# A transformer layer on one core: the start of the program is put in another order, and the first sequence's k leaves through ScalarE's queue

## Chip, cores and metric

The kernel runs on one core of one Trainium2 chip. The metric is the device time in microseconds of one execution; lower is better. A core has five engines that run side by side and meet only at semaphores: TensorE (PE; its weight loads are listed as PEld), VectorE (DVE), ScalarE (ACT), GpSimd (POOL) and SyncE (SP), which here only issues DMAs. Every engine executes its own instructions strictly in the order in which they are written, so a wait holds up all that stands behind it on that engine.

## What is computed

One adaLN transformer layer over x of shape (16, 512, 128), that is 16 sequences b of 512 tokens with 128 features. The reference, cut to what matters:

```python
mod = (silu(c) @ wmod).reshape(16, 6, 1, -1)          # sa, ca, ga, sb, cb, gb, one set per sequence
ga, gb = clamp_abs(ga, 0.25), clamp_abs(gb, 0.25)      # sign kept
h = layernorm(x) * (1 + ca) + sa
q, k, v = h @ wq.T + bq, h @ wk.T + bk, h @ wv.T + bv  # 16 heads of 8
scores = q k^T * 8**-0.5, only |i - j| <= 32
x = x + ga * (softmax(scores) @ v @ wo.T + bo)
h = layernorm(x) * (1 + cb) + sb
top 2 of 8 experts by softmax(h @ gate_w.T); experts and one shared: (silu(h s w1) * (h s w3)) @ w2
x = x + gb * (sum over the experts)
```

## The kernel before

**Stages.** The work goes sequence by sequence. Attention of sequence b runs beside the experts of sequence b-2. `fill()` holds by hand the order of all instructions of sequences 0 to 4 (with the experts of 0 to 2), `body(b, par)` is the repeated order for b = 5 to 11, `drain()` is the rest. Each engine has its own three lists, written out call by call, and nothing reorders them at run time.

**The prologue** stands ahead of `fill()`. SP issues eight loads of weights and of x (lines 282 to 288 and `load_x(0)` at 294), then the experts' weights w13 and w2 (lines 431, 432), then `load_x(1)`. The first seven share one semaphore `w_in`, and whoever needs one of them waits for all seven (112). From the condition `ct` ACT makes a tanh (line 1138), DVE makes silu from it (`cth` line 1671, `csl` line 1673), PE multiplies it with `wmod` (lines 2638 and 2641), DVE writes `mod` (lines 1680, 1681), PE multiplies that with the projection weights (line 2644), and DVE makes the biases `bqk` and `bvs` of all sequences (lines 1874 to 1876). DVE also forms the low parts `wql` of the split weights (lines 1675, 1676), and from lines 1878 to 1890 `mrow`, the rows of ga, gb and ga*bo, which go to DRAM (`put_rows`, lines 427, 428) and come back broadcast over the partitions as `brow`, `arow`, `grow` (lines 302, 310, 318).

**The first layernorm.** `statistics` (line 1691) and `moments` (line 1701) on DVE, `spread_var`, `inverse`, `shift`, `normal` on POOL (lines 665, 674, 680, 706), `flip` on PE (line 2659), `high_h1` on ACT (line 1160), `low_h1` on DVE (line 1707). Then PE projects q, k, v, each as three products of high and low parts (lines 2622 to 2624). ACT writes the high parts `qh`, `kh` (lines 1169, 1176), DVE the low parts `ql`, `kl` (lines 1717, 1725).

**Rearrangement of q and k through DRAM.** `put_q`, `put_ql`, `put_k`, `put_kl` (lines 327, 336, 345, 354) store them to `q_scr` and `k_scr`; `load_q` (line 364, four DMAs) and `load_k` (line 380, three DMAs) bring them back as `q4` and `k4`, for blocks 0 to 7 (h = 0) and 8 to 15 (h = 1) of the sequence apart. `load_q` waits until all three q stores have landed, `load_k` until all three k stores have, and the first ones also until the unused rows of `q4` are zero (`z_in`). Rows 96 to 127 of `q4` hold ones (`ones_q`, line 767, once for each h), and those of `k4` hold the window mask.

**Attention.** For each block n of 32 queries: `scores` on PE (line 2697), `maximum` on DVE (line 1738), `probabilities` on ACT (line 1184), `turn_p` on DVE (line 1755), `values` on PE (line 2720). Two score banks alternate. `add_bias` on POOL (line 696) needs `brow`. `warm(n)` on PE issues n matmuls whose result is not used (line 2629).

**Experts.** `scaled` (line 737) and `scaled_low` (line 743) on POOL, `scaled_high` (line 1206) on ACT, `expert` on PE, `half_silu` (line 1835) and `combine` (line 1844) on DVE, `down` on PE (line 2765). `expand_v` (line 715) on POOL spreads v.

## Time and profile before

| what | value |
|---|---|
| median of 3 runs | 700.81 us (695.68, 700.81, 701.35) |
| the profiled execution, its own time | 696.14 us |
| the profiled execution, its span | 694.1 us |
| PE busy | 653.3 us, 94% of the span |
| DVE, ACT, POOL busy | 599.7, 554.5, 566.2 us (86%, 80%, 82%) |
| DMA | 127.79 MB, mean 184 GB/s |

The time of an execution is its span and some 2 us around it (696.14 against 694.1). The span begins with the first instruction and ends with the last. The profile gives for every instruction its start and its duration; a bracket behind a row says how long the engine stood idle before it, and what ended that. Of a DMA the profile shows how long its issue took on the queue and, for some, how long it was from issue to landing. The granted clock of TensorE is 1.00 at 2.4 GHz and 0.50 at 1.2 GHz.

### The profile page before, as it was taken

The page shows a single profiled execution, that of the slowest core. Times are in us where ns is not written, and L with a number is a line of the kernel's source. Part 1 is how long each engine was busy: PE and PEld are TensorE (multiplying, and loading weights), DVE is VectorE, ACT ScalarE, POOL GpSimd, SP SyncE. Part 2 cuts the span into 40 slices and gives each one's busy share as a digit, 9 for nine tenths or more (in the row PEclk, how much of TensorE's full clock was granted, in tenths as well). Part 3 has the DMA queues.
Part 4 walks back from the last instruction along what each step waited for, and adds up shares of the span by engine and source line. Part 5 has one row for each costly group of instructions (what it writes and reads, how often), then busy time and mean ns, then how long its engine had stood idle before and what let it go on. Part 6 is the DMA issues. An engine that isn't in the chain of part 4 may idle for free. (4 is left out here: it accounts for less than half of the span.)

```text
span 694.1 us, 19396 instructions
## 1 busy us (share of the span) xinstructions
PE 653.3 (94%) x6075; PEld 560.8 (81%) x6075; DVE 599.7 (86%) x1568; ACT 554.5 (80%) x2458; POOL 566.2 (82%) x667
## 2 busy tenths in 40 slices
PE   6488889999999999999999999999999999999897
PEld 5277777888888888888888888888888888887685
DVE  6737778999898989999999999899989999897685
ACT  3258787989888888989898889899899898986352
POOL 6430619999988979899998989898999999898684
PEclk8669988999999999999999999999999999999999
DMA  5567788786787787786878777887868787633231
GB/s 175 157 143 192 164 211 219 197 232 165 178 241 196 202 219 190 189 231 159 224 205 227 190 201 205 228 201 191 201 190 210 207 209 221 157 101 99 77 129 31
DMA packets 193862, 127.79 MB, mean 184 GB/s; under 512 B 110640, under 2 KB 170720, under 8 KB 193632
## 3 DMA queue, kind: packets, MB, share of 16 engines
q1 hardware_dynamic: 193760, 126.56, 69.2%
q8 instruction: 48, 0.79, 0.5%
q14 instruction: 54, 0.44, 0.2%
HBM read 96.36 MB, written 30.17 MB: 182 GB/s over the span
## 5 line engine op out<-in xcount | busy, mean ns | idle before, releaser
L1184 ACT ACTIVATE p<-ps_s,nmx 128x96 f32<-128x96 f32 x1024 | 330.9, 344 | 34.9 <-DVE nmx L1738 33.0
L1184 ACT ACTIVATION_READ_ACCUMULATOR p<-ps_s,nmx 128x1 f32 x1024 | 216.2, 211 | 0.0
L737 POOL TENSOR_TENSOR xs<-h,sbc 128x512 f32<-128x512 f32 x128 | 165.5, 1300 | 18.9 <-DMA sbc<-s_scr 17.6
L1738 DVE TENSOR_REDUCE nmx<-ps_s 128x4 f32<-128x384 f32 x256 | 137.2, 548 | 37.0 <-PE ps_s L2697 36.8
L2697 PEld LDWEIGHTS ps_s<-k,q 128*128 128x128 f32 x1024 | 140.1, 197 | 34.1 <-DMA k<-k_scr 14.2
L743 POOL TENSOR_TENSOR xl<-xs,xh 128x512 fp32r<-128x512 f32 x120 | 153.4, 1283 | 17.2 <-ACT xh L1206 17.1
L2697 PE MATMUL ps_s<-k,q 128*128 128x96 f32 x1024 | 145.4, 277 | 18.7 <-DMA k<-k_scr 13.3
L2765 PE MATMUL ps_Y<-w2s,g 128*128 128x128 f32 x1152 | 153.5, 279 | 0.4 <-DVE g L1844 0.4
L2765 PEld LDWEIGHTS ps_Y<-w2s,g 128*128 128x128 f32 x1152 | 140.4, 192 | 5.6 <-DVE g L1844 0.8
L1755 DVE STREAM_TRANSPOSE pt<-p 128x384 f32<-128x384 f32 x256 | 133.5, 551 | 0.8 <-ACT p L1184 0.3
L1206 ACT ACTIVATE xh<-xs 128x512 fp32r<-128x512 f32 x128 | 79.9, 636 | 34.0 <-POOL xs L737 33.5
L1835 DVE SCALAR_TENSOR_TENSOR th<-th,ps_A 128x512 f32<-128x512 f32 x136 | 91.7, 674 | 15.1 <-ACT th L1227 13.9
L1227 ACT ACTIVATE th<-ps_A 128x512 f32<-128x512 f32 x136 | 82.5, 607 | 24.5 <-PE ps_A L2624 23.3
L1844 DVE TENSOR_TENSOR g<-th,ps_B 128x512 f32<-128x512 f32 x136 | 91.9, 676 | 1.7 <-PE ps_B L2624 0.3
L2622 PE MATMUL ps_A<-xh,w13h 128*128 128x512 f32 x136 | 63.3, 466 | 2.0 <-DVE th L1835 1.0
L2720 PE MATMUL ps_O<-pt,vd 128*32 128x96 f32 (+2 forms) x2304 | 64.4, 243 | 0.0
L715 POOL TENSOR_TENSOR vd<-vt,bmask 128x1024 f32<-128x1024 f32 x32 | 60.6, 1896 | 0.5 <-DVE vt L1733 0.5
L2622 PE MATMUL ps_B<-xh,w13h 128*128 128x512 f32 x136 | 55.3, 407 | 2.6 <-DVE g L1844 2.6
L2720 PEld LDWEIGHTS ps_O<-pt,vd 128*32 128x32 f32 x2304 | 44.2, 111 | 16.3 <-issue 6.0
L2624 PE MATMUL ps_B<-xl,w13h 128*128 128x512 f32 x136 | 53.7, 395 | 0.0
L2624 PE MATMUL ps_A<-xl,w13h 128*128 128x512 f32 x136 | 53.7, 395 | 0.0
L2623 PE MATMUL ps_A<-xh,w13l 128*128 128x512 f32 x136 | 53.6, 394 | 0.0
(138 smaller groups left out, 1010.8 us busy)
## 6 DMA issues: line engine op xcount, KB each, us to landing
sbc<-s_scr SPq DMA_DIRECT2D x64, 512.0 KB, 6.2
k<-k_scr SPq DMA_DIRECT2D x64, 384.0 KB
q<-q_scr SPq DMA_DIRECT2D x128, 96.0 KB
k<-k_scr SPq DMA_DIRECT2D x32, 336.0 KB
q_scr<-qh SPq DMA_DIRECT2D x32, 256.0 KB, 3.7
k_scr<-kh SPq DMA_DIRECT2D x32, 256.0 KB, 2.9
xr<-x SPq DMA_DIRECT2D x16, 256.0 KB, 3.1
q_scr<-ql SPq DMA_DIRECT2D x16, 256.0 KB, 3.7
```

What stands on the lines that cost most here:

```text
L737: nc.gpsimd.tensor_tensor(xs[:, n % 2], h2[:, par], sbc[:, n - 1], ALU.mult).then_inc(xs_d, 1)
L743: nc.gpsimd.tensor_tensor(xl[:, n % XRING], src, xh[:, n % XRING].bitcast(F32), ALU.subtract).then_inc(xl_d, 1)
L1184: last = nc.scalar.activation(p[:, n % PRING, gg, :], ps_s[:, n % 2, MK * gg:MK * gg + MK], ACT.Exp, bias=nmx[:, n, gg:gg + 1], accum_out= ...
L1738: nc.vector.tensor_reduce(nmx[:, n, :], ps_s[:, n % 2, 0:ACC].rearrange("p (g k) -> p g k", g=HG), AX.X, ALU.max, negate=True).then_inc(mx ...
L1755: nc.vector.transpose(pt[:, n % TRING].rearrange("p g r q -> p (g r q)"), p[:, n % PRING].rearrange("p g k -> p (g k)")).then_inc(tr_d, 1)
L1835: nc.vector.scalar_tensor_tensor(th[:, par], th[:, par], 1.0, banks(b, n)[0], ALU.add, ALU.mult).then_inc(v_d, 1)
L1844: nc.vector.tensor_tensor(g[:, par], th[:, par], banks(b, n)[1], ALU.mult).then_inc(g_d, 1)
L2622: mm(dst, wh, xh, start=True, stop=False)
L2624: return mm(dst, wh, xl, start=False, stop=True)
L2697: last = mm(ps_s[:, n % 2, MK * gg:MK * gg + MK], heads[:, h, gg, nl], k4[:, h, gg, :, MB * nl:MB * nl + MB], start=gg == 0, stop=gg == HG ...
L2720: last = mm(ps["O"][r, MB * n0:MB * n0 + MB * cnt], vd[:, kb, gg].rearrange("p j d -> p (j d)"), src, start=kb == 0 and run is runs[0], st ...
L2765: last = mm(ps["Y"][:, QB * a:QB * a + QB], g[:, par, QB * a:QB * a + QB], w2s[:, e, :], start=n == 0 and a == 0, stop=n == NX - 1, skip_g ...
```

## The change

Nothing is computed in another way. In the prologue SP loads `ct` first, then the first x, `wmod` and the projection weights, each with a semaphore of its own (`ct_in`, `x_in[0]`, `wm_in`, `wq_in`); the four small ones keep `w_in`, whose full count is 64 now. ACT makes the tanh and the high parts of the weights before the window mask, and `ones_q` is split: POOL writes it for h = 0 behind the first layernorm, ACT for h = 1 behind the k stores. DVE takes the statistics of the first x ahead of the condition, and makes the rows `mrow` (`make_rows`) after the first projections. The zeroing of `q4` is shared: DVE does half of h = 0, POOL the other half and all of h = 1. The memset of the middle of `k4` stands behind `low_h1(0)`. PE issues 8 matmuls on `ident` where it issued 14.

On SP `put_rows` moves from ahead of the first q store to behind the first loads of q4 and k4. `put_k(0, 0)` and `put_kl(0, 0)` leave SP; ACT issues the same three DMAs in their place (`send_k`, `send_kl`). For sequences 1 to 4 neighbours in the hand-written lists of all five engines trade places, and the `warm` calls of PE are set anew: 96 warm matmuls in `fill` where there were 107 (the first eight ahead of `project_v(0)` and those of the prologue stay). `body` and `drain` are unchanged.

The diff, cut to its core (the reordered neighbours of sequences 1 to 4 are left out but for a few):

```diff
...
-            sp.dma_start(wqf, wqkv).then_inc(w_in, 16)
-            sp.dma_start(ct[:], cT).then_inc(w_in, 16)
-            sp.dma_start(wm, wmod).then_inc(w_in, 16)
+            sp.dma_start(ct[:], cT).then_inc(ct_in, 16)
+            sp.dma_start(xr[:, 0], x[0:1].rearrange("o (a p) d -> p (o a) d", p=128)).then_inc(x_in[0], 16)
+            sp.dma_start(wm, wmod).then_inc(wm_in, 16)
+            sp.dma_start(wqf, wqkv).then_inc(wq_in, 16)
...
-                    sp.wait_ge(z_in[h], 1)
+                    sp.wait_ge(z_in[h], 2 - h)
...
-                    sp.wait_ge(z_in[0], 1)
+                    sp.wait_ge(z_in[0], 2)
...
-            load_x(0)
             sp.dma_start(w13f, w13).then_inc(e_in, 16)
             sp.dma_start(w2f, w2).then_inc(e_in, 16)
             load_x(1)

             def fill():

-                put_rows()
+                load_x(2)
                 put_q(0, 0)
                 put_ql(0, 0)
-                put_k(0, 0)
-                put_kl(0, 0)
                 load_q(0, 0, 0)
                 load_k(0, 0, 0)
+                put_rows()
                 load_bias(0)
                 load_ga(0)
                 load_q(0, 1, 0)
                 load_k(0, 1, 0)
-                load_gb(0)
-                load_bias(1)
-                load_x(2)
                 put_q(1, 1)
...
-            ones_q(0)
+            spread_var(0, l1, ln1)
+            inverse(0, l1, ln1)
+            shift(0, l1, ln1)
+            normal(0, l1, ln1)
+            pool.wait_ge(l1["xn"], NQB)
+            ones_q()
             const(nc.gpsimd.memset(bmask[:], 1.0))
             keep(bmask[:], [[-32, HJ]], 0, 1, val=0.0)
             keep(bmask[:], [[32, HJ]], 31, -1, val=0.0)
             const(nc.gpsimd.iota(iota8[:], [[1, NE]], base=0, channel_multiplier=0,
                                  allow_small_or_imprecise_dtypes=True))
-            ones_q(1)
-            spread_var(0, l1, ln1)
-            inverse(0, l1, ln1)
-            shift(0, l1, ln1)
-            normal(0, l1, ln1)
+            nc.gpsimd.memset(q4[0:KROWS, 0, 2:4].bitcast(F32), 0.0).then_inc(z_in[0], 1)
+
+            def clear_q():
+
+                nc.gpsimd.memset(q4[0:KROWS, 1].bitcast(F32), 0.0).then_inc(z_in[1], 1)

             def fill():

-                spread_var(1, l1, ln1)
                 expand_v(0, 0)
                 expand_v(0, 1)
+                clear_q()
+                spread_var(1, l1, ln1)
+                inverse(1, l1, ln1)
+                shift(1, l1, ln1)
                 add_bias(0)
-                inverse(1, l1, ln1)
+                normal(1, l1, ln1)
                 gate_wo(0)
...
+                scaled_low(0, 0, 0)
                 route_both(0)
                 route_weights(0)
-                scaled_low(0, 0, 0)
+                expand_v(2, 0)
...
+            act.wait_ge(ct_in, 16)
+            nc.scalar.activation(cth[:], ct[:], ACT.Tanh, scale=0.5).then_inc(s_th, 1)
+            act.wait_ge(wq_in, 16)
+            nc.scalar.activation(wqh[:, 0], wqf[:, 0], ACT.Copy, scale=SCALE)
+            nc.scalar.activation(wqh[:, 1:3], wqf[:, 1:3], ACT.Copy).then_inc(s_wh, 1)
...
+            def ones_q():
+
+                act.wait_ge(cst, IDENT)
+                nc.scalar.activation(q4[KROWS:128, 1].rearrange("p g n j q -> p (g n j) q"),
+                                     ident[KROWS:128, KROWS:128].unsqueeze(1).to_broadcast([MB, HG * HB * HJ, MB]),
+                                     ACT.Copy).then_inc(q_one[1], 1)
+
+            def send_k(b, par):
+
+                act.wait_ge(k_h, b + 1)
+                for role in (0, 1):
+                    nc.scalar.dma_start(k_scr[par, :, role].rearrange("j r s -> r j s"),
+                                        kh[:].bitcast(F32)).then_inc(k_scr_w, 16)
+
+            def send_kl(b, par):
+
+                act.wait_ge(k_l, b + 1)
+                nc.scalar.dma_start(k_scr[par, :, 2].rearrange("j r s -> r j s"), kl[:].bitcast(F32)).then_inc(k_scr_w, 16)
...
+                copy_w2()
+                send_k(0, 0)
+                send_kl(0, 0)
+                ones_q()
                 copy_w13()
-                copy_w2()
...
-            nc.vector.memset(q4[0:KROWS, 0].bitcast(F32), 0.0).then_inc(z_in[0], 1)
-            nc.vector.memset(k4[KROWS:128, :, :, 1].bitcast(F32), 0.0)
-            dve.wait_ge(s_th, 1)
-            nc.vector.scalar_tensor_tensor(cth[:], cth[:], 1.0, ct[:], ALU.add, ALU.mult).then_inc(s_sv, 1)
-            dve.wait_ge(s_sv, 1)
-            nc.vector.tensor_scalar(csl[:], cth[:], 0.5, None, ALU.mult).then_inc(s_sl, 1)
-            dve.wait_ge(s_wh, 1)
-            nc.vector.scalar_tensor_tensor(wql[:, 0], wqf[:, 0], SCALE, wqh[:, 0].bitcast(F32), ALU.mult, ALU.subtract)
-            nc.vector.tensor_tensor(wql[:, 1:3], wqf[:, 1:3], wqh[:, 1:3].bitcast(F32), ALU.subtract).then_inc(s_wl, 1)
-
-            dve.wait_ge(s_mod, 1)
-            pm = ps["M1"][:, 0:4 * B].rearrange("p (k b) -> p k b", k=4)
-            nc.vector.tensor_copy(mod[:, 0:4:2], pm[:, 0:4:2])
-            nc.vector.tensor_scalar(mod[:, 1:4:2], pm[:, 1:4:2], 1.0, None, ALU.add).then_inc(s_md, 1)
-
+            nc.vector.memset(q4[0:KROWS, 0, 0:2].bitcast(F32), 0.0).then_inc(z_in[0], 1)
...
             statistics(0, l1, ln1)
             moments(0, l1, ln1)
+            dve.wait_ge(s_th, 1)
+            nc.vector.scalar_tensor_tensor(cth[:], cth[:], 1.0, ct[:], ALU.add, ALU.mult).then_inc(s_sv, 1)
+            dve.wait_ge(s_sv, 1)
+            nc.vector.tensor_scalar(csl[:], cth[:], 0.5, None, ALU.mult).then_inc(s_sl, 1)
+            dve.wait_ge(s_wh, 1)
+            nc.vector.scalar_tensor_tensor(wql[:, 0], wqf[:, 0], SCALE, wqh[:, 0].bitcast(F32), ALU.mult, ALU.subtract)
+            nc.vector.tensor_tensor(wql[:, 1:3], wqf[:, 1:3], wqh[:, 1:3].bitcast(F32), ALU.subtract).then_inc(s_wl, 1)
+            dve.wait_ge(s_mod, 1)
+            pm = ps["M1"][:, 0:4 * B].rearrange("p (k b) -> p k b", k=4)
+            nc.vector.tensor_copy(mod[:, 0:4:2], pm[:, 0:4:2])
+            nc.vector.tensor_scalar(mod[:, 1:4:2], pm[:, 1:4:2], 1.0, None, ALU.add).then_inc(s_md, 1)
+            dve.wait_ge(w_in, 64)
             dve.wait_ge(s_sa, 1)
             nc.vector.tensor_scalar(bqk[:, 0], ps["M0"][:, 0:B], bia[:, 0:1], SCALE, ALU.add, ALU.mult)
             nc.vector.tensor_scalar(bqk[:, 1], ps["M0"][:, B:2 * B], bia[:, 1:2], None, ALU.add)
             nc.vector.tensor_scalar(bvs[:], ps["M0"][:, 2 * B:3 * B], bia[:, 2:3], None, ALU.add).then_inc(s_bq, 1)
-            dve.wait_ge(s_bo, 1)
...
             low_h1(0)
+            nc.vector.memset(k4[KROWS:128, :, :, 1].bitcast(F32), 0.0)
             low_q(0)
             low_k(0)

             def fill():

+                turn_v(0)
                 statistics(1, l1, ln1)
+                make_rows()
+                split_w13()
                 moments(1, l1, ln1)
-                split_w13()
-                turn_v(0)
-                clear_q()
                 maximum(0, 0)
...
-            for i in range(14):
+            for i in range(8):
                 mm(ps["A"][:, 0:128], ident[:], ident[:], start=True, stop=True)
-            pe.wait_ge(w_in, 112)
-            pe.wait_ge(s_wh, 1)
+            pe.wait_ge(wm_in, 16)
...
+            pe.wait_ge(s_wh, 1)
...
                 warm(3)
                 scores(0, 3)
                 flip(1, l1, ln1, "M1")
+                values(0, 0)
+                scores(0, 4)
                 warm(3)
-                scores(0, 4)
-                warm(6)
+                project_q(1)
                 scores(0, 5)
-                project_q(1)
+                warm(3)
+                scores(0, 6)
                 project_k(1)
-                scores(0, 6)
-                warm(5)
+                values(0, 1)
+                values(0, 2)
+                warm(2)
                 scores(0, 7)
...
```

SP, from behind the experts' weights to the second half's q: first as the order of before has it (`xr` is x, `m_scr` and `b_scr` take the rows of `mrow`, `brow` and `arow` are those rows coming back).

```order
L294 DMA xr<-x 128x4x128
L427 DMA m_scr<-mrow 16x256
L428 DMA b_scr<-mrow 16x128
L327 DMA q_scr<-qh 32x4x512 x2
L336 DMA q_scr<-ql 32x4x512
L345 DMA k_scr<-kh 32x4x512 x2
L354 DMA k_scr<-kl 32x4x512
L364 DMA q<-q_scr 24x32x32 x4
L380 DMA k<-k_scr 96x4x224
L380 DMA k<-k_scr 96x4x256 x2
L302 DMA brow<-b_scr 128x128
L310 DMA arow<-m_scr 128x128
```

And the same stretch of SP in the changed kernel:

```order
L295 DMA xr<-x 128x4x128 x2
L328 DMA q_scr<-qh 32x4x512 x2
L337 DMA q_scr<-ql 32x4x512
L365 DMA q<-q_scr 24x32x32 x4
L381 DMA k<-k_scr 96x4x224
L381 DMA k<-k_scr 96x4x256 x2
L428 DMA m_scr<-mrow 16x256
L429 DMA b_scr<-mrow 16x128
L303 DMA brow<-b_scr 128x128
L311 DMA arow<-m_scr 128x128
L365 DMA q<-q_scr 24x32x32 x4
```

The three k stores are gone from SP, and the two stores of the rows now stand behind the seven loads of q and k instead of ahead of the q stores.

DVE, from its third instruction to the biases: first before (`cth` and `csl` are the condition, `wql` the low weights, `l_st` and `l_mv` the statistics of x).

```order
L1668 MEMSET q 96x4096
L1669 MEMSET k 32x8x256
L1671 SCALAR_TENSOR_TENSOR cth<-cth,ct 128x16
L1673 TENSOR_SCALAR csl<-cth 128x16
L1675 SCALAR_TENSOR_TENSOR wql<-pt,wqh 128x128
L1676 TENSOR_TENSOR wql<-pt,wqh 128x256
L1680 COPY mod<-ps_M 128x2x16
L1681 TENSOR_SCALAR mod<-ps_M 128x2x16
L1691 BN_STATS l_st<-xr 128x6 x4
L1699 MEMSET spare 128x1
L1701 BN_AGGR l_mv<-l_st 128x2 x4
L1874 TENSOR_SCALAR bqk<-ps_M,bia 128x16
```

And the same stretch of DVE in the changed kernel:

```order
L1695 MEMSET q 96x2048
L1704 BN_STATS l_st<-xr 128x6 x4
L1712 MEMSET spare 128x1
L1714 BN_AGGR l_mv<-l_st 128x2 x4
L1900 SCALAR_TENSOR_TENSOR cth<-cth,ct 128x16
L1902 TENSOR_SCALAR csl<-cth 128x16
L1904 SCALAR_TENSOR_TENSOR wql<-pt,wqh 128x128
L1905 TENSOR_TENSOR wql<-pt,wqh 128x256
L1908 COPY mod<-ps_M 128x2x16
L1909 TENSOR_SCALAR mod<-ps_M 128x2x16
L1912 TENSOR_SCALAR bqk<-ps_M,bia 128x16
```

The statistics stand ahead of the condition now, the first memset is half as long, and the memset of `k` is gone from this stretch.

## Rows read from the trace of the kernel before

**Rows 1.** Windows: busy us of each engine (instructions), granted clock, DMA share, GB/s.

```profile
10.00:20.00 10.00, 7.76 (x30) 6.13 (x31) 6.51 (x26) 0.48 (x1) 4.78 (x9) 0.54 0.18 63
...
80.00:100.00 20.00, 18.44 (x185) 15.82 (x184) 16.22 (x55) 15.90 (x86) 5.76 (x13) 0.91 0.86 214
...
240.00:640.00 400.00, 397.01 (x3873) 340.65 (x3877) 367.15 (x994) 353.23 (x1587) 366.21 (x419) 1.00 0.74 194
```

**Rows 2.** Timeline of 0 to 22 us: start, duration, engine, line, operation.

```profile
0.79 0.40 SPq L282 DMA_DIRECT2D pt<-wqkv  x1
...
1.99 3.47 DVE L1668 MEMSET q<- 96x4096 f32 x1 [0.80 <-issue]
...
6.57 0.22 ACT L1138 ACTIVATE cth<-ct 128x16 f32<-128x16 f32 x1 [0.35 <-DMA p<-borow]
...
7.53 3.59 POOL L767 CAST q<-ident 32x4096 fp32r<-32x4096 f32 x1
7.72 3.44 DVE L1671 SCALAR_TENSOR_TENSOR cth<-cth,ct 128x16 f32<-128x16 f32 x1
...
11.51 1.86 PE L2638 MATMUL ps_M<-csl,pt 128*128 128x16 f32 x8 [3.79 <-DVE csl L1673]
...
13.62 0.47 DVE L1691 BATCH_NORM_STATS2 l_st<-xr 128x6 f32<-128x128 f32 x2
...
14.27 1.46 PE L2644 MATMUL ps_M<-mod,pt 128*128 128x16 f32 x6
...
14.61 0.28 DVE L1701 BATCH_NORM_AGGREGATE l_mv<-l_st 128x2 f32<-128x6 f32 x3
...
16.89 2.06 POOL L706 TENSOR_SCALAR l_xn<-xr,l_rstd,l_nm 128x128 f32<-128x128 f32 x4
...
19.52 0.69 ACT L1160 ACTIVATE hh<-ps_M,mod 128x512 fp32r<-128x512 f32 x1 [12.23 <-PE ps_M L2659]
...
21.05 0.50 PE L2622 MATMUL ps_M<-hh,wqh 128*128 128x512 f32 x1 [0.28 <-DVE hl L1707]
```

**Rows 3.** DMA issues, 0 to 45 us: KB, median us from issue to landing.

```profile
pt<-wmod SPq DMA_DIRECT2D x1, 384.0 KB, 3.3
pt<-wqkv SPq DMA_DIRECT2D x1, 256.0 KB, 2.7
...
ct<-cT SPq DMA_DIRECT2D x1, 8.0 KB, 2.5
```

**Rows 4.** Timeline of 22 to 40 us: q and k stored, loaded, first scores.

```profile
22.76 1.29 SPq L327 DMA_DIRECT2D q_scr<-qh  x2
...
24.74 1.27 SPq L345 DMA_DIRECT2D k_scr<-kh  x2
...
26.78 3.38 SPq L364 DMA_DIRECT2D q<-q_scr  x4
...
30.27 2.04 SPq L380 DMA_DIRECT2D k<-k_scr  x3
...
37.91 1.94 PE L2697 MATMUL ps_s<-k,q 128*128 128x96 f32 x8 [12.67 <-DMA k<-k_scr]
```

**Rows 5.** Waits of the DMA queue, 0 to 60 us: total, times, longest.

```profile
SPq L362 <- DMA q_scr<-ql: 0.5, 1, 0.5
```

**Rows 6.** Timeline: first use of brow, flip of sequence 1, block 8 of sequence 0.

```profile
38.36 1.27 POOL L696 TENSOR_TENSOR xr<-xr,brow 128x512 f32<-128x512 f32 x1 [5.88 <-DMA brow<-b_scr]
...
44.88 1.10 PE L2659 MATMUL ps_M<-ident,l_xn 128*128 128x128 f32 x4
...
54.28 0.62 PE L2697 MATMUL ps_s<-k,q 128*128 128x96 f32 x4 [1.31 <-ACT p L1184]
```

**Rows 7.** Windows of the warm matmuls alone (line 2629): PE, PEld, clock, DMA, GB/s.

```profile
80.00:100.00 20.00, 6.10 (x23) 4.51 (x23) 0.91 0.86 214
```

**Rows 8.** The page's groups: busy us, mean ns, idle before.

```profile
L1835 DVE SCALAR_TENSOR_TENSOR th<-th,ps_A 128x512 f32<-128x512 f32 x136 | 91.7, 674 | 15.1 <-ACT th L1227 13.9
```

**Rows 9.** Waits of 86 to 120 us.

```profile
POOL xs L737 <- DMA sbc<-s_scr: 7.7, 1, 7.7
```

358 lines of the change are left out of this document (175 added, 183 removed).

## The prediction

> **What bounds the kernel now.** I first read the windows [rows 1]. From 240 to 640 us PE is busy 397.01 of 400 us at full clock: there PE sets the pace, the change leaves that part alone, and its length cannot move. The reader should next see that 80 to 100 us is another regime: PE shows 18.44 of 20 us, but 6.10 of them are warm matmuls [rows 7], so useful work is only 12.3. Up to about 120 us the end is set by chains of waits. Whatever the first sequence gains there should reach the end of the program one for one, since PE's useful work is the same in both kernels.
>
> So I followed the chain of the prologue in the timeline [rows 2]. Tanh starts at 6.57, released by the last of the seven loads that share a semaphore. Silu's first instruction, 16 columns wide, takes 3.44 us on DVE: it ends with POOL's copy of the ones (7.53 + 3.59 = 11.12). PE starts on the condition at 11.51 after 3.79 us of idleness, DVE comes to x only at 13.62, the moments end at 14.89, POOL's normalized x at 18.95, `hh` starts at 19.52 and the projections at 21.05. From there the chain goes through DRAM [rows 4]: q stores at 22.76, q loads at 26.78, k loads at 30.27, and the first scores at 37.91, released by the k load.
>
> **The front, step by step.** SP's first DMA starts at 0.79 [rows 2], and an issue takes 0.4. With `ct` first it lands at 0.79 + 2.5 = 3.3, the first x (256 KB, like the projection weights before) at 1.2 + 2.7 = 3.9 [rows 3]. `wmod` landed 3.3 after its issue with 264 KB ahead of it; it has as much ahead now and lands near 5.0. The projection weights now have 648 KB ahead of them; 384 KB more than the 256 KB ones cost about 1.5 us (0.9 for the later issue, 0.6 for the longer landing), so I put them 1.0 behind `wmod`'s own 5.0 to 5.4, at 6.2.
>
> - DVE: statistics and moments took 14.89 - 13.62 = 1.27; from 3.9 they end at 5.2. The half memset (3.47 for the whole one, so some 1.75 from 1.99) ends at 3.75, before x is there. Silu is 3.44 before, with POOL's copy beside it; the copy now stands behind the first layernorm, and the small DVE instructions near it are of the order of 0.2, so `csl` is ready at 5.7 instead of 11.4. Worst case, POOL's small `spread_var` and power delay it by 1.
> - PE: the 8 matmuls on `ident` end near 5.1. The condition's product took 1.86 at the low clock (10 to 20 us: 0.54 [rows 1]); 0.95 to 1.86 now, so it ends at 6.7 to 7.6.
> - DVE forms `wql` before it reads that product. The high parts (384 columns on ACT, like `hh` 0.69 for 512) come at 6.9, `wql` takes another 0.7 and may wait for up to two short POOL instructions: 7.6 to 8.5. `mod` (two small instructions, some 0.3) is there at 8.2, the middle.
> - PE: the next product is 1.46 at the low clock or 0.75 at the full one. From its end (14.27 + 1.46 = 15.73) to `hh` was 3.8, with DVE's biases, the product with `wo`, three warm matmuls and the flip in it, at the low clock and with waits for POOL's x: the upper end. The flip alone is 1.10 at the low clock [rows 6]; I put PE's share at 2.8 of the 3.8, halved at full clock, so 2.4 is the lower end. Sum from 8.2: 11.3 (full clock) to 13.5 (low clock). POOL's normalized x needs 18.95 - 14.89 = 4.1 after the moments: 9.3, so it is no longer the last.
>
> `hh` starts at 11.3 to 13.5 against 19.52: a gain of 8.2 to 6.0. PE's idle gaps become shorter than 3.79, but work stays sparse, and in 10 to 20 us a busy share of 7.76 in 10 went with 0.54 of the clock. I take 7.0, nearer the low clock.
>
> **Behind the front.** Let T be the start of the projections (21.05 before). The memset in the middle of `k4` (half the length of the removed one, 1.8) lies behind `low_h1` while PE multiplies: hidden, and it costs at most 0.5 if not. `make_rows` (eight small instructions) would be on the path at T now, where before it ended beside the flip; it moves behind, where DVE waits for scores. The k stores: SP loses three issues, 1.27 + 0.6. But the first q load waits for the last q store to land, and of that wait 0.5 was left even after the k issues [rows 5]; the saving is 0.5 at the very most, and since the store still has to land I count 0.1. The k stores now start after `copy_w2`, some 1.2 us behind `kh`, are issued by T + 5.5 and land by T + 8.5, ahead of the k load at T + 9.2. ACT then has the ones (4096 columns, for which POOL took 3.59) and `w13h` (2304 columns, at most 3.1 at `hh`'s rate): done by T + 12.2, DVE's split of w13 (at most 3.4 at that rate) by T + 15.6. The scores come at T + 16.9 (37.91 - 21.05): covered, with 1.3 left by these upper ends. If ACT's issues were slow, this is the first cover to go, one for one.
>
> The Trainium skill (DMA: Bandwidth & Descriptors, Issuing engines are not separate DMA queues) says that DMAs from different engines run on the same 16 DMA engines and interleave, and that a second issuer saves issue time only. By that rule the store through ACT gains no transfer time, and the sum has 0 here instead of 0.1; the trace's 0.5 us of wait left at the q load agrees.
>
> **What is late next.** `put_rows` now stands behind seven loads. The queue's order shows: `brow`, issued after the k loads (30.27 + 2.04), is there only at 38.36, with k itself [rows 4, 6]. The rows' stores will wait in the same way to about T + 17.3, `brow` is issued then, lands 2.5 to 4.3 later, and `add_bias` (1.27) with `normal(1)` (at most 2.06, like the first) ends at T + 23.1 to T + 24.9. The flip of sequence 1 was at 44.88 = T + 23.8. So it costs 0 to 1.1; I take 0.5. The second half of q and k is issued by T + 24 and lands by T + 28 to T + 31; block 8 ran at 54.28 = T + 33.2 and waited for ACT, not for data. Free.
>
> POOL's ones (3.6) end near T + 0.5 in the new order, beside `low_h1`, which reads one operand from PSUM. DVE's `th` instruction has the same form and takes 674 ns on average beside a busy POOL [rows 8]; so no cost. The Trainium skill (SBUF — State Buffer, Who interferes with whom) says that a DVE instruction with two SBUF inputs and a POOL instruction that reads SBUF exclude each other, and one with a single SBUF input is free; the 3.44 us of silu beside POOL's 3.59 agree. By that rule the removed collision is worth 3.2 us, within the front's sum, and `low_h1` stays free. Were it blocked too, 0.9 would be lost.
>
> **The new order of sequences 1 to 4.** `expand_v(2, 0)` moves into POOL's 7.7 us of waiting for the experts' weights [rows 9] and out of the crowded stretch behind it. It has 1024 columns; `add_bias` with 512 takes 1.27, so up to some 2 less there. 11 warm matmuls of some 0.27 us (6.10 / 23, [rows 7]) go. Both ends: +3 if a stage is pushed behind a wait, -4. I take -1.0, for the POOL move alone.
>
> **Sum.** -7.0 - 0.1 + 0.5 - 1.0 = -7.6, so the profiled execution of 696.14 becomes 688.5. The runs shown lie at two levels, 695.68 beside the profiled 696.14, and 700.81 beside 701.35. The new kernel may fall at either; I name the middle of the two (698.5) less 7.6: 690.9, say 691.
>
> **Rivals.**
> 1. *Forecast*: the front passes through, 6 to 9 saved. 0.46.
> 2. *More*: full clock in the front (8.2) and a real gain in the fill, 9 to 13 saved, about 685.5 on the profile's level. For it: short gaps of PE. Against: the clock of rows 1. 0.18.
> 3. *Part is given back*: low clock in the projections too (six products, +1), the rows behind the loads delay the flip, and the second half of k comes late (each +1 to +2). 2 to 5 saved, about 692.5. For it: `brow`'s 5.88 us of waiting. 0.27.
> 4. *The change doesn't do what it says*: the first scores are bound by transfers that start no earlier, 0 to 2 saved, 695. Against: the DMA share is only 0.18 in 10 to 20 us, the transfers wait for PE and DVE. 0.04.
> 5. *Slower*: fewer warm matmuls let the granted clock fall to 1.2 GHz in the fill. In 80 to 100 us, at 0.91, PE works 18.44; at 0.50 that is 33.6 in 20, +13.6. From 11 us of low clock in addition the gain is used up; at 25 us, +17, the time is 705.5. For it: the clock is 0.91 there despite the warm ones. Against: 96 of 107 remain. 0.05.
>
> About 1% (7 us) is what a measurement of this kernel can tell from no change. Case 1 lies above it with three quarters, case 2 wholly: faster 0.52. Slower by over 1% is most of case 5, 0.04; the rest 0.44. The range: the upper end is case 3 at the upper level (700.81 - 4), the lower is case 2 at the lower level (696.14 - 11.5): 684.5 to 697.
>
> **What would show it.** In the new profile `csl` near 5.7, `hh` between 11 and 13.5, projections near 14 and first scores near 31; SP's first q load 4 us behind the first q store, no wait of the first scores but for k; `brow` some 20 us after T; block 8 waiting for ACT. Wrong if `hh` starts after 14, if the first scores wait for POOL or ACT, if block 8 waits for k, if the clock is below 0.7 in more than 10 us between 50 and 120, or if the gain at the first scores isn't there at 240 us.

## The result, and the profile after

| | kernel before | changed kernel |
|---|---|---|
| median of 14 runs each, us | 698.58 (693.25 to 705.39) | 692.82 (689.31 to 698.38) |
| profiled execution, us (span) | 696.14 (694.1) | 693.66 (691.9) |
| ratio, 95% interval | | 0.993 [0.9901, 0.9959] |

The ratio is a gain of 4.9 us on 698.58, with 2.9 to 6.9 as the interval's ends. The forecast of 691 is 1.8 below the median and the range of 684.5 to 697 holds it, but the gain was forecast as 7.6, and less than 1% came. The base of the forecast, 698.5, was the middle of two levels that four runs seemed to show; the 14 runs of the kernel before lie spread from 693.25 to 705.39 without two levels, so that their median is 698.58 was luck. The ratios are of fast runs alone, and of the profiled executions that of e5_sums, 702.42 us, is a slow one. The two profiled executions differ by only 2.5 us: that of the kernel before lies 2.4 below its own median, that of the changed one 0.8 above. Positions inside the two traces are therefore compared up to a given point, and totals by the medians.

The timeline of the changed kernel, 0 to 15.6 us, is the front that [rows 2] show of before.

```profile
0.79 0.40 SPq L282 DMA_DIRECT2D ct<-cT  x1
...
1.67 3.78 PE L2658 MATMUL ps_A<-ident 128*128 128x128 f32 x16 [1.67 <-POOL ident L657]
...
4.19 0.87 DVE L1704 BATCH_NORM_STATS2 l_st<-xr 128x6 f32<-128x128 f32 x4 [0.86 <-DMA xr<-x]
...
5.39 0.14 DVE L1900 SCALAR_TENSOR_TENSOR cth<-cth,ct 128x16 f32<-128x16 f32 x1
...
5.57 0.17 DVE L1902 TENSOR_SCALAR csl<-cth 128x16 f32<-128x16 f32 x1
...
5.89 1.86 PE L2662 MATMUL ps_M<-csl,pt 128*128 128x16 f32 x8 [0.45 <-DVE csl L1902]
...
7.76 1.74 POOL L704 TENSOR_SCALAR l_xn<-xr,l_rstd,l_nm 128x128 f32<-128x128 f32 x4
...
8.65 1.46 PE L2669 MATMUL ps_M<-mod,pt 128*128 128x16 f32 x6
...
9.56 3.60 POOL L765 CAST q<-ident 32x4096 fp32r<-32x4096 f32 x1
...
13.56 0.69 ACT L1165 ACTIVATE hh<-ps_M,mod 128x512 fp32r<-128x512 f32 x1 [2.92 <-PE ps_M L2685]
...
14.28 0.75 DVE L1720 SCALAR_TENSOR_TENSOR hl<-ps_M,mod,hh 128x512 fp32r<-128x512 f32 x1 [3.53 <-ACT hh L1165]
...
15.08 0.51 PE L2647 MATMUL ps_M<-hh,wqh 128*128 128x512 f32 x1 [0.53 <-DVE hl L1720]
```

The reader should see three things. Silu's first instruction takes 0.14 us instead of 3.44, with POOL's copy of the ones now behind the first layernorm. `csl` ends at 5.74 instead of 11.4. And the condition's product takes 1.86 us, exactly as before at the low clock, although it starts 0.44 us after the last matmul on `ident`. `hh` starts at 13.56, 5.96 earlier than before; PE, by its bracket, was the last to be ready.

The same timeline further on, 15 to 47 us, answers to [rows 4] and [rows 6]; T, the start of the projections, is now 15.08.

```profile
15.51 1.76 DVE L1916 MEMSET k<- 32x2048 f32 x1 [0.48 <-issue]
...
16.80 1.29 SPq L328 DMA_DIRECT2D q_scr<-qh  x2
...
17.52 1.50 ACTq L1245 DMA_DIRECT2D k_scr<-kh  x2
...
18.14 0.61 SPq L337 DMA_DIRECT2D q_scr<-ql  x1
...
20.57 3.79 POOL L713 TENSOR_TENSOR vd<-vt,bmask 128x1024 f32<-128x1024 f32 x2 [4.64 <-DVE vt L1746]
...
21.91 3.49 SPq L365 DMA_DIRECT2D q<-q_scr  x4
22.53 1.97 DVE L1882 TENSOR_SCALAR p<-p 16x256 f32<-16x256 f32 x1
...
24.30 3.65 POOL L797 MEMSET q<- 96x4096 f32 x1
...
24.98 3.11 DVE L1886 TENSOR_SCALAR p<-p 16x256 f32<-16x256 f32 x1
...
28.78 2.54 DVE L1895 TENSOR_TENSOR w13l<-sbc,w13h 128x2304 fp32r<-128x2304 f32 x1
...
32.08 1.94 PE L2723 MATMUL ps_s<-k,q 128*128 128x96 f32 x8 [12.35 <-DMA k<-k_scr]
...
35.91 1.28 POOL L694 TENSOR_TENSOR xr<-xr,brow 128x512 f32<-128x512 f32 x1 [2.48 <-DMA brow<-b_scr]
...
38.58 0.72 PE L2685 MATMUL ps_M<-ident,l_xn 128*128 128x128 f32 x4
...
46.60 0.62 PE L2723 MATMUL ps_s<-k,q 128*128 128x96 f32 x4 [1.00 <-ACT p L1189]
```

The first scores come 5.83 earlier (37.91 to 32.08) and wait for k, as before. From the first q store to the first q load it is now 5.11 us (21.91 - 16.80), before 4.02 (26.78 - 22.76). The DMA issues of 0 to 34 us say why (KB each, median us from issue to landing): each store that shares its time with the other queue's takes about a microsecond longer than the 2.5 to 2.7 that the same transfers took before.

```profile
q_scr<-qh SPq DMA_DIRECT2D x2, 256.0 KB, 2.5
k_scr<-kh ACTq DMA_DIRECT2D x2, 256.0 KB, 3.5
...
q_scr<-ql SPq DMA_DIRECT2D x1, 256.0 KB, 3.7
k_scr<-kl ACTq DMA_DIRECT2D x1, 256.0 KB, 3.7
```

Sequence 4 (timeline, 170 to 185 us; the last row is from 176 to 190) is where this execution loses most of the lead that had grown in between.

```profile
170.57 1.39 SPq L410 DMA_DIRECT2D r_scr<-rst  x2
...
174.71 0.59 SPq L417 DMA_DIRECT2D rt<-r_scr  x1
...
181.17 0.69 DVE L1777 TENSOR_TENSOR o<-ps_O,rt 128x512 f32<-128x512 f32 x1 [4.10 <-DMA rt<-r_scr]
...
181.78 0.68 DVE L1871 TENSOR_TENSOR yt<-ps_Y,grow 128x512 f32<-128x512 f32 x1
...
182.60 2.05 PE L2791 MATMUL ps_Y<-w2s,g 128*128 128x128 f32 x8 [3.17 <-DVE yt L1871]
...
189.19 0.99 PE L2723 MATMUL ps_s<-k,q 128*128 128x96 f32 x8
```

DVE waits 4.10 us for `rt`, the softmax's scale, on its way through DRAM. `yt`, which frees PE's next output, stands behind it, and PE waits 3.17 us. Then PE runs slowly: the granted clock is 0.50 from 181.4 to 188.2 us. e3_k_sp (one of the experiments below) has the same code in this sequence, nearly the same wait, and no low clock at this place (its timeline, 176 to 190 us):

```profile
180.81 0.69 DVE L1777 TENSOR_TENSOR o<-ps_O,rt 128x512 f32<-128x512 f32 x1 [3.66 <-DMA rt<-r_scr]
...
182.24 1.13 PE L2791 MATMUL ps_Y<-w2s,g 128*128 128x128 f32 x8 [2.73 <-DVE yt L1871]
...
186.41 0.99 PE L2723 MATMUL ps_s<-k,q 128*128 128x96 f32 x8
```

The same eight passes take 1.13 us instead of 2.05, and from them to the next scores it is 4.17 us instead of 6.59. So 2.4 us of the 3.0 that the changed kernel loses from sequence 4 to 5 go with the low clock behind the wait. e3_k_sp loses 0.8 there. A few of the windows of the changed kernel, for the clock, with the 400 us of [rows 1] last:

```profile
0.00:10.00 10.00, 7.89 (x34) 7.05 (x34) 4.47 (x18) 5.15 (x8) 5.73 (x23) 1.00 0.75 243
...
180.00:200.00 20.00, 17.40 (x165) 15.92 (x166) 16.09 (x44) 13.69 (x64) 14.56 (x19) 0.83 0.79 217
240.00:640.00 400.00, 395.79 (x3825) 337.67 (x3823) 363.40 (x969) 346.65 (x1555) 362.32 (x413) 1.00 0.73 191
```

How far the changed kernel is ahead of the kernel before is read best from the first row maximum (the DVE reduce at line 1738 before, 1751 after) of a sequence. The table gives the lead in us over the profiled execution of before.

| | seq. 0 | seq. 1 | seq. 2 | seq. 4 | seq. 5 | seq. 8 | seq. 15 |
|---|---|---|---|---|---|---|---|
| changed kernel | 5.8 | 7.6 | 10.8 | 9.5 | 6.5 | 6.4 | 2.3 |
| new front, old order (e2_front) | 6.1 | 4.3 | 4.6 | 4.5 | 4.9 | 6.1 | 3.1 |
| old front, new order (e8_lists) | -0.4 | 1.7 | 5.1 | 4.6 | 3.2 | 1.7 | -1.8 |
| k stores on SP (e3_k_sp) | 5.2 | 8.0 | 11.3 | 9.6 | 8.8 | 8.8 | 6.3 |
| 14 matmuls on `ident` (e4_warm14) | 8.4 | 8.6 | 12.0 | 11.3 | 10.7 | 11.0 | 8.9 |

So the front gives 5.8, the new order of sequences 1 to 4 adds 5 by sequence 2, and 4.3 of the 10.8 are gone by sequence 5, 2.4 of them with the low clock at sequence 4. Whether the other executions of the changed kernel have that stretch is not known. Among the other kernels with the new order it is in the profiles of e1_finish, e5_sums, e8_lists and e11_gaps, and not in those of e3_k_sp, e4_warm14, e6_w14_ksp, e7_all and e10_warm20. Every row loses a further 1.8 to 5.0 us between sequences 5 and 15, where all these kernels have the same code: the one thing common to the rows is the profiled execution of before, quicker than its median. That this is the reason is likely and not shown. So I read leads up to sequence 5 and totals from the ratios.

### The profile page after: what moved, and what is told of

It reads as the page before. It is cut to its first block and busy times, and to the rows that moved or that the text cites. A ratio compares the mean times of both kernels' runs of the same rounds, so it can differ in the third digit from the quotient of the medians.

```text
span 691.9 us, 19353 instructions
## 1 busy us (share of the span) xinstructions
PE 652.8 (94%) x6052; PEld 557.7 (81%) x6052; DVE 596.2 (86%) x1567; ACT 557.9 (81%) x2459; POOL 565.6 (82%) x668
## 5 line engine op out<-in xcount | busy, mean ns | idle before, releaser
L1848 DVE SCALAR_TENSOR_TENSOR th<-th,ps_A 128x512 f32<-128x512 f32 x136 | 91.9, 675 | 14.0 <-ACT th L1232 12.5
L2746 PEld LDWEIGHTS ps_O<-pt,vd 128*32 128x32 f32 x2304 | 42.9, 110 | 16.2 <-issue 6.6
```

What stands on the lines that cost most here:

```text
L1848: nc.vector.scalar_tensor_tensor(th[:, par], th[:, par], 1.0, banks(b, n)[0], ALU.add, ALU.mult).then_inc(v_d, 1)
L2746: last = mm(ps["O"][r, MB * n0:MB * n0 + MB * cnt], vd[:, kb, gg].rearrange("p j d -> p (j d)"), src, start=kb == 0 and run is runs[0], st ...
```

## The experiments

Each kernel was timed in turn with the kernel before on the same chip: e1 to e4 on one chip (its median of before is 696.45), e5 to e8 on a second (696.98), e9 to e11 on a third (696.66). Each diff is against the changed kernel, except that of e8_lists.

**One part undone or doubled.** Which part of the change holds the gain?

### e1_finish

```diff
+                finish(1)
                 scale_o(3)
-                finish(1)
```

> The changed kernel with one call moved back on VectorE: finish(1) stands ahead of combine's neighbour scale_o(3) again, so it no longer waits behind it for the DMA of rt (4.10 us of idleness in the changed kernel's trace, then PE idle for 3.17 us, released by yt, and a granted clock of 0.5 for 6.8 us from 181 us on). Theory A (the fourth sequence gives back about 4 us of a lead of 10 because of this order): the PE wait released by yt is gone, the lead over the kernel before at the first scores of sequence 5 is 8.5 to 10.5 us instead of 6.5, and the ratio is 0.987 to 0.991. Rival B (the late rt itself is the cost, whatever stands behind it: attn_out needs it anyway): PE waits about as long a few instructions later, the lead stays at 6 to 7.5 us, the ratio stays at 0.993. Rival C (the low clock there is not caused by the wait): the wait goes and the low clock stays, a lead of 7.5 to 8.5.

Measured: 691.9 us, 0.992 [0.9891, 0.995], the same as the changed kernel's 0.993. Theory A (a ratio of at most 0.991 and a lead of 8.5 or more at sequence 5, measured 4.8) did not come. The order is that of before again, and the wait stayed. In the waits of 160 to 200 us PE now stops at the product of the attention's output instead of at `down`:

```profile
DVE o L1777 <- DMA rt<-r_scr: 3.3, 1, 3.3
...
PE ps_M L2766 <- issue: 1.7, 1, 1.7
```

`rt` itself is late; what stands behind it decides which instruction of PE waits, and for how long. As in the changed kernel the clock was low behind that wait, for 3.4 us from 187.2.

### e2_front

```diff
 new prologue, stores through ACT: kept
-new lists of SP, POOL, DVE and PE for sequences 1 to 4, and their warm matmuls
+those of the kernel before
```

> The front alone: prologue and first sequence as changed (k through ScalarE, rows behind the loads), but for sequences 1 to 4 the lists and warm matmuls of before. Theory A (the front is worth 6 us and the new lists add to it before sequence 2 and lose it again in sequence 4): first scores at 32.1, a lead of 5.5 to 7.5 at the first scores of sequence 2 (10.8 with the new lists), the same 5 to 7 at sequence 5, and a ratio of 0.991 to 0.994, like the full change. Rival B (the lead of 10.8 comes with the front, since the clock rises earlier): 9 to 11 at sequence 2 here too, and a ratio of 0.987. Rival C (the lists and the front need each other): a new wait in sequence 0 or 1, a lead under 4, a ratio of 0.996 or more.

Measured: 692.72 us, 0.9944 [0.9923, 0.9965]. The front alone is worth 3.9 us of 696.45, against 4.9 for the whole, 0.0004 outside the ratios of theory A; the lead at sequence 2 is 4.6, below its 5.5. Its trace adds something: with the same code in the first 15 us this execution had the condition's product quick, and `hh` at 11.83 (timeline, 0 to 12 us):

```profile
5.99 1.04 PE L2662 MATMUL ps_M<-csl,pt 128*128 128x16 f32 x8 [0.70 <-DVE csl L1902]
...
7.54 0.84 PE L2669 MATMUL ps_M<-mod,pt 128*128 128x16 f32 x6
...
11.83 0.69 ACT L1165 ACTIVATE hh<-ps_M,mod 128x512 fp32r<-128x512 f32 x1 [1.50 <-PE ps_M L2685]
...
31.82 1.94 PE L2723 MATMUL ps_s<-k,q 128*128 128x96 f32 x8 [13.43 <-DMA k<-k_scr]
```

A part of that was lost in the projections, which had the low clock here (`hh` to the first q store 3.93 us, in the changed kernel 3.24), and 0.79 more between the q store and the first scores (16.07 against 15.28), so these are only 0.26 earlier than in the changed kernel.

### e3_k_sp

```diff
+ SP:  put_k(0, 0); put_kl(0, 0)   behind put_ql(0, 0)
- ACT: send_k(0, 0); send_kl(0, 0)
```

> The changed kernel with the first sequence's three k stores issued by SP again, behind the q stores; ScalarE keeps its order without them. Theory A (the other queue spares no time at the first scores, since the q load waits for the last q store to land and the k load for the transfers): first scores within 0.5 us of 32.1, ratio to before unchanged within 0.002. In the changed trace the q load came 5.1 us after the first q store against 4.0 before: if the k data on the second queue delays the landing of q, the q load comes here at 4.0 to 4.5 us. Rival B (the k store through ScalarE is worth SP's 1.9 us of issue time): first scores 1 to 2 us later, 33.1 to 34.1. Rival C (it costs time): first scores 0.5 to 1.2 us earlier.

Measured: 690.91 us, 0.9923 [0.9901, 0.9946]: not told apart from 0.993 by the time, as theory A had it. The trace does tell: `ql` lands in 2.5 us again, and the wait of SP in front of the q load (waits of the DMA queue, 0 to 60 us) is 0.2. In the changed kernel that line read 3.5 us in two waits, the longest 3.1.

```profile
SPq L363 <- DMA q_scr<-ql: 0.2, 1, 0.2
```

From q store to q load it is 4.01 us again. This number is steady over all thirteen profiles of this study: 5.03 to 5.14 in the five kernels that store k through ACT, 4.00 to 4.03 in the eight that store it on SP, the kernel before among them. From q store to first scores it is 15.3 to 16.1 in the former and 14.4 to 15.2 in the latter. In this execution `hh` (13.81) and the projections were slower than in the changed kernel's, so its first scores, at 32.66, are not earlier.

### e4_warm14

```diff
-            for i in range(8):
+            for i in range(14):
                 mm(ps["A"][:, 0:128], ident[:], ident[:], start=True, stop=True)
```

> The changed kernel with 14 matmuls on the identity at PE's start where it has 8. In the changed trace PE's products with the condition take as long as in the kernel before at the low clock (1.86 and 1.46 us), so the front got the low-clock end of its estimate. Theory A (six matmuls fewer leave PE at 1.2 GHz until 14 us; with 14 it goes up at 7 to 8 us as it did before): PE starts on the condition at 7.7 instead of 5.9, but the product with the projections takes 0.75, the flip half, and hh starts at 13.0 to 13.9, against 13.56: no gain, no loss. Rival B (the clock stays low in the gaps all the same): hh at 15.0 to 15.5, the whole lead shrinks by 1.5 to 1.8. Rival C (the clock is up and stays up): hh at 12.3 or earlier.

Measured: 687.27 us, 0.9867 [0.9834, 0.9899]; this interval does not touch that of the changed kernel, 0.9901 to 0.9959, nor that of e3_k_sp, which was timed on the same chip, 0.9901 to 0.9946. Theory A expected no gain; what came is rival C. The timeline, 0 to 30 us:

```profile
1.67 4.74 PE L2658 MATMUL ps_A<-ident 128*128 128x128 f32 x28 [1.67 <-POOL ident L657]
...
6.24 0.96 PE L2662 MATMUL ps_M<-csl,pt 128*128 128x16 f32 x8
...
7.67 0.84 PE L2669 MATMUL ps_M<-mod,pt 128*128 128x16 f32 x6
...
10.79 0.69 ACT L1165 ACTIVATE hh<-ps_M,mod 128x512 fp32r<-128x512 f32 x1 [0.44 <-PE ps_M L2685]
...
29.53 1.94 PE L2723 MATMUL ps_s<-k,q 128*128 128x96 f32 x8 [12.57 <-DMA k<-k_scr]
```

The product starts 0.35 us later, behind the six added matmuls, and ends 0.55 earlier; `hh` gains 2.77 and the first scores 2.55. Durations of 0.96 against 1.86 for the same eight passes are the two levels of the clock, 2.4 and 1.2 GHz. The six matmuls that the change took out of the front, as if they were idle filling, set the level at which the path behind them ran. They would not have done so in the kernel before, which has all 14: its product took 1.86 too. There PE was idle for 3.79 us in front of the product, and the clock, up from 7.3 us, had fallen again at 10.7. So the six are worth something only on the front with that gap closed.

Position by position this execution is ahead of the changed one by 2.6 us at sequence 0, by 1.8 at sequence 4 and by 4.2 at sequence 5. The last step is the low clock of the changed execution at sequence 4, which this one doesn't have. That the six matmuls are the reason for that too is not shown: e3_k_sp has 8 and doesn't have it either.

**Where the lead of sequence 4 goes, and the parts together.**

### e5_sums

```diff
 SP, sequence 3, on top of e1_finish:
+                put_sums(3)
                 load_q(4, 1, 0)
...
-                put_sums(3)
```

> The changed kernel with finish(1) ahead of scale_o(3) on VectorE, and put_sums(3) ahead of load_q(4, 1, 0) on SP. With finish(1) moved alone the wait for rt stayed (3.3 us on DVE) and PE waited 1.7 us at attn_out instead of at down. Theory A (the sums stand behind a q load whose issue takes 7 to 8 us there, and the late rt is what sequence 4 gives back): rt is issued 2 us or more earlier after the first scores of sequence 4, the DVE wait for it falls under 1.5 us, the lead does not shrink between the first scores of sequences 4 and 5 by more than 0.7 us, and the ratio is 0.987 to 0.990. Rival B (the q load, now later, takes over as what is waited for: block 8 of sequence 4 waits for it): the lead shrinks by 1.5 to 3 all the same.

Measured: 693.7 us, 0.9945 [0.9922, 0.9968]: no gain. In its waits, 160 to 200 us, SP stands at the sums and waits for ACT to produce them, and DVE's wait is still there:

```profile
SPq L410 <- ACT rst L1199: 4.6, 1, 4.6
...
DVE o L1777 <- DMA rt<-r_scr: 3.8, 1, 3.8
```

Theory A, that the place of the stores in SP's list makes `rt` late, is refuted. Measured from the sequence's first row maximum, `rt` is issued at +10.7 us in the changed kernel, +11.6 here and +10.7 before. `o`, which needs it, ran at +17.2 in the changed kernel and at +16.0 before, and there DVE stood idle in front of it as well (timeline of before, 180 to 192 us):

```profile
189.52 0.69 DVE L1764 TENSOR_TENSOR o<-ps_O,rt 128x512 f32<-128x512 f32 x1 [2.34 <-issue]
```

The view names no releaser, but `rt` landed at 189.43, 5.26 us after its issue; in the changed kernel it took 6.38. So the kernel before has the wait too, 1.8 us shorter, and what differs is 1.1 us of landing and DVE's earlier arrival. What the sums wait for on ACT and PE was not separated further.

### e6_w14_ksp and e7_all

```diff
 e6_w14_ksp = range(14) of e4_warm14 + k stores on SP of e3_k_sp
 e7_all     = e6_w14_ksp + the two edits of e5_sums
```

> The changed kernel with 14 matmuls on the identity and the first k stores on SP again: both single edits together. Theory A (each has its own gain: the clock in the front 2.7 us, the q store's landing 0.4 to 1.0): hh at 10.5 to 11.5, the q load 4.0 us after the first q store, first scores at 28.8 to 29.3 (29.52 with 14 matmuls alone), ratio 0.983 to 0.987. Rival B (hh at 10.79 with 14 matmuls was the luck of one run; with 8 it was 11.82 to 14.34 in four kernels with the same front): hh at 12 to 14 here, first scores at 31 to 33, a ratio near 0.992. Rival C (k by either queue is the same once the transfers are what ends last): first scores at 29.5 or later with hh at 10.8.

> All together: 14 matmuls on the identity, k stores on SP, finish(1) ahead of scale_o(3), put_sums(3) ahead of load_q(4, 1, 0). Theory A: a lead over before of 11 to 13 us at the first scores of sequence 2 that is still there at sequence 5, and a ratio of 0.980 to 0.985, the fastest of all. Rival B (PE's pace behind sequence 5 takes the lead back): a lead of 11 or more at sequence 5, and a ratio of 0.987 or more.

Measured: e6_w14_ksp 687.71 us, 0.9859 [0.9818, 0.99]; e7_all 689.22 us, 0.9869 [0.9825, 0.9914]. Against e3_k_sp (0.9923) the six matmuls bring 0.6% again. Against e4_warm14 the place of the k store brings nothing that the time can show. The reordering of sequences 3 and 4 brings nothing in either combination. In e6_w14_ksp the ratio is theory A's, while `hh` at 11.65 and the first scores at 29.48 come 0.15 and 0.18 us behind its ranges. e7_all fits neither of its theories: the ratio is over 0.985 and the lead at sequence 5 is 9.6.

### e8_lists

```diff
 against the kernel before:
-old lists of SP, POOL, DVE and PE for sequences 1 to 4, and their warm matmuls
+those of the changed kernel
 prologue of the kernel before: kept
```

> The kernel before with the new lists and warm matmuls for sequences 1 to 4, and the front of before. Theory A (the lists win 3 to 5 us before sequence 2 by themselves and give 1.5 to 4 back in sequence 4): first scores at 37.9, a lead of 2.5 to 5 at the first scores of sequence 2, 0 to 2.5 at sequence 5, a ratio of 0.996 to 1.000. Rival B (the new lists fit only the new front): no lead at sequence 2, a loss at sequence 5, a ratio of 1.001 to 1.006.

Measured: 698.28 us, 0.9996 [0.9966, 1.0026]. With the old front the new order is worth nothing to within 2.4 us, although its profiled execution is 5.1 us ahead at sequence 2 (the table above), the 5 us that the changed kernel gains there too. At sequence 5 it is 3.2 ahead, after the same wait for `rt` (3.60 us) and 3.4 us of low clock from 186.5.

**How many matmuls, and must they be first?**

### e9_front14, e10_warm20, e11_gaps

```diff
 e9_front14 = e2_front + range(14) + k stores on SP
 e10_warm20 = e6_w14_ksp with range(20)
 e11_gaps   = e3_k_sp, and in front of the products with mod and with the biases, each:
+            for i in range(2):
+                mm(ps["A"][:, 0:128], ident[:], ident[:], start=True, stop=True)
```

> The new front with 14 matmuls on the identity and k through SP, and the lists of before for sequences 1 to 4. The lists alone gave a ratio of 0.9996, with 14 matmuls and k on SP the new lists gave 0.9859. Theory A (the lists are worth nothing at the end, the front everything): hh at 10.8 to 11.7, a lead of 8 to 10 at the first scores of sequence 2 (14.5 with the new lists), ratio 0.985 to 0.989. Rival B (the lists are worth their lead once the front is short): ratio 0.990 to 0.993.

> 14 to 20 matmuls on the identity, k on SP, all else as changed. Theory A (the gain is in the clock, and 14 already get it; more only hold PE): PE starts on the condition at 7.7 to 8.5 instead of 7.1, hh at 11.5 to 12.5, ratio 0.986 to 0.990. Rival B (more hold the clock up longer): hh at 11 or earlier and the second product under 0.9 us, ratio 0.982 to 0.985.

> 8 matmuls on the identity at the start as in the changed kernel, and two more of them in each of two gaps of PE (ahead of the wait for mod, and ahead of the wait for the biases); k on SP. Theory A (what counts is that PE has no gaps while the front runs, wherever the matmuls stand): hh at 10.8 to 12.0, first scores under 30.5, ratio 0.985 to 0.989. Rival B (it must be ahead of the condition's product): the products keep their 1.86 and 1.46 us, hh at 13.5 to 14.5, ratio 0.991 to 0.994, like the three k stores on SP alone (0.9923).

Measured: e9_front14 689.45 us, 0.9897 [0.9857, 0.9938]; e10_warm20 686.96 us, 0.9867 [0.9827, 0.9906]; e11_gaps 689.11 us, 0.9878 [0.9835, 0.9921].

e9_front14 is ahead by 9.6 us at sequence 2 and by 8.4 at sequence 5, where e6_w14_ksp with the new order is ahead by 14.5 and 12.5. Its ratio lies between the ranges of theory A and rival B, so what the new order is worth with the quick front stays open. With 20 the matmuls delay the path themselves (condition at 8.11, `hh` at 12.66, in e6_w14_ksp 7.11 and 11.65), and the time doesn't change beyond the intervals between 14 and 20 (theory A, with `hh` 0.16 behind its range). With matmuls in the gaps instead, the first product in the profile stays at the low level and the second is nearly as slow (1.30 us, against 1.46 low and 0.84 with 14 in front; timeline, 5 to 16 us), and `hh` is the latest of all new fronts:

```profile
6.02 1.86 PE L2662 MATMUL ps_M<-csl,pt 128*128 128x16 f32 x8 [0.57 <-DVE csl L1902]
...
9.79 1.30 PE L2671 MATMUL ps_M<-mod,pt 128*128 128x16 f32 x6
...
14.82 0.69 ACT L1167 ACTIVATE hh<-ps_M,mod 128x512 fp32r<-128x512 f32 x1 [4.43 <-PE ps_M L2689]
```

The products are near rival B's, and `hh` is later than even B had it; the ratio is theory A's. It lies between those of 8 and of 14 matmuls and its interval overlaps both, so whether the gaps help in most executions stays open. This very execution took 689.64 us with the latest `hh`, and that of e2_front 693.01 with an early one: in single executions the place of `hh` doesn't settle the total. What is shown is that the six matmuls shorten the front and that they shorten the kernel; that all of the second comes by way of the first is not.

Over all profiles: with 8 matmuls and a path otherwise alike, `hh` starts at 13.56, 14.34, 13.81, 13.60 and once at 11.83 us, and the ratios lie from 0.992 to 0.9945; with 14 it starts at 10.79, 11.65, 11.04 and 11.11, and the ratios with the new order are 0.9859 to 0.9869.

## Why the prediction was right in part

By its own steps:

- **What bounds the kernel, and the front's chain: right.** The part at full clock is unchanged in kind (PE busy 395.79 of 400). `ct` was used at 2.61, x at 4.19 (predicted 3.3 and 3.9); the moments ended at 5.47 (5.2), `csl` at 5.74 (5.7), `mod` at 8.07 (8.2), and POOL's x at 9.50 (9.3), no longer the last. The price of the collision, 3.4 us for silu, was read rightly. That the gain of the first sequence reaches the end "one for one" is neither refuted nor shown: 5.8 us at the first scores against 4.9 (2.9 to 6.9) here, 8.4 against 9.3 (7.0 to 11.6) in e4_warm14, but 6.1 against 3.9 (2.4 to 5.4) in e2_front.
- **"I take 7.0, nearer the low clock": mis-sized.** `hh` started at 13.56, at the low clock's end of the bounds of 11.3 to 13.5 and 0.06 beyond it: a gain of 5.96. The failed step is "the 8 matmuls on `ident` end near 5.1", which counted the removal of six of them as nothing. They ended at 5.45, and the product ran at the low level; with 14 it runs at the high one and `hh` gains 8.73 against before. I had both prices of the product and 0.54 as the clock of that stretch, and did not ask what in the change sets the clock. e4_warm14 and e6_w14_ksp put the six matmuls at 0.6% of the whole, 4.4 us; 2.55 of it shows at the first scores, and the rest has no shown cause. For the gap between forecast and result this term gives 1.0 of the 2.7 us.
- **"`make_rows` moves behind, where DVE waits for scores": right in sign, short in size.** It took 2.9 us before and ran from 21.15 to 28.85 now. Two of its instructions on 16 x 256 took 1.97 and 3.11 us beside POOL's `expand_v` and its memset. So the split of w13 ended at 31.32, T + 16.2 instead of T + 15.6, and of the cover of 1.3 us 0.8 was left. No cost, by luck of the margin.
- **"The saving is 0.5 at the very most ... I count 0.1": wrong in sign for the q load.** The k stores landed ahead of the k load, as said, but `ql` landed in 3.7 us instead of 2.5 because k's data shared its time, and the first q load moved from 4.02 to 5.11 behind the store. At the first scores little of it is left: from T they came at 17.0 us against 16.9. The Trainium skill (DMA: Bandwidth & Descriptors, Issuing engines are not separate DMA queues) says that such DMAs share the same 16 engines; the trace agrees, and shows that sharing can cost what the rule only calls no gain. The half memset of `k4`, priced at "at most 0.5 if not" hidden, sat in front of `ql` (15.51 to 17.27), whose data were ready at 18.04; SP was busy with the two issues of `qh` until 18.09, so it cost nothing and has 0.05 us of cover left. In the total e3_k_sp and e6_w14_ksp leave the store's effect inside the intervals.
- **Rows behind the loads, +0.5: it was 0.** `brow` was issued at T + 17.3, as predicted, but partly by luck: where I had the stores of the rows wait for the transfers ahead of them, SP waited 1.4 us for the late end of `make_rows` and then 2.6 for the rows to land. It landed 3.4 us after its issue, in the middle of the bounds, and the flip of sequence 1 was at T + 23.5 against T + 23.8 before, inside the 23.1 to 24.9. Block 8 waited for ACT. Case 3's "second half of k comes late" did not happen.
- **"I take -1.0, for the POOL move alone": between 0 and 2.7, not resolved.** e8_lists saves 0.3 (-1.8 to 2.4), the changed kernel against e2_front 1.0, e6_w14_ksp against e9_front14 2.6, each within the intervals. What I had not forecast is its shape in the changed kernel's profile: 5 us ahead at sequence 2, and most of it back by sequence 5, where DVE waits 4.10 us for `rt` and PE then has 6.8 us of low clock. In e3_k_sp, without that low clock, 8.8 of 11.3 are still there.
- **The clock rival did not come.** By the letter of my last paragraph it should have ("the clock is below 0.7 in more than 10 us between 50 and 120"): the changed kernel has 10.2 us of the low level from 92.6 on and the end of another stretch. But the kernel before has 13.6 there (the granted clock of 50 to 120 us is 0.91 after and 0.90 before), so the mark was set without reading its own value. In single executions the clock can take lead away: e2_front had 6.1 us at the first scores and 4.3 at sequence 1, and in between, at 52 to 58 us, its granted clock was 0.65, where the kernel before, 6 us later, had 0.96. And the changed kernel's low stretch at sequence 4 lies outside the 50 to 120 us that I watched.

Sum by the measured terms: -6.0 for `hh` (-5.8 at the first scores with the store's loss in it), 0 for the rows, 0 to -2.7 for the order, against -4.9 [-6.9, -2.9] measured. In size it was case 3, part is given back (2 to 5 saved), but by none of the three mechanisms that I had put there: the projections ran at full clock (0.39 to 0.40 us a matmul), the flip wasn't delayed, the second half of k wasn't late. The forecast of 691 lies close to 692.82 partly by luck, as the range is wide and the base was a lucky one. The kernels with 14 matmuls and the new order reached case 2, "full clock in the front" and 9 to 13 saved: `hh` gained 8.73 (8.2 in that case), and the ratios of 0.9859 to 0.9869 are 9.1 to 9.8 us.

## What to carry to other kernels

Matmuls that compute nothing are part of the path when useful ones follow: before removing them, find the first useful product in the trace and ask at which clock it runs, for here leaving out six of them cost 3 us of chain and 0.6% of the time, though in front of a gap of 3.79 us they had been worth nothing. When a store moves to another queue, compare the landing of every transfer that now shares its time, not the issue slots saved. A lead inside the pipeline can be lost again, so follow it sequence by sequence to the stretch in which one engine is always busy, and read the granted clock wherever it shrinks before you blame the wait that stands there.
